# Gated cross-attention block with a two-of-eight expert layer on one core: the order of work on four engines, the pieces of GpSimd's subtractions and the queues of the last stores are changed

## The chip, the cores and the metric

The kernel runs on one core of one Trainium2 chip. The metric is the device time of one launch in microseconds (us). The core's engines run side by side, each in its own program order, and wait for one another through semaphores: TensorE (PE in the rows; PEld is its weight load), VectorE (DVE), ScalarE (ACT), GpSimd (POOL) and SyncE (SP, which here only issues transfers; SPq, ACTq and POOLq are the queues).

## The reference

2048 tokens of width 256 come in 32 sequences of 64. `ctx` has the same shape, no entry is masked, and both gates are scalars.

```python
def xattn(x, ctx):
    q, k_new, v_new = x @ wq.T, x @ wk.T, x @ wv.T
    k, v = concat([ctx, k_new]), concat([ctx, v_new])      # per sequence: 64 old and 64 new keys
    return softmax(q @ k.T / 16) @ v @ wo.T

def ffn(x):                                                # 8 experts, the 2 best of a softmax router
    combine = top_2(softmax(x @ gate_w.T))
    y = sum_e combine[:, e] * ((silu(x @ fc1[e].T) * (x @ fc2[e].T)) @ proj[e].T)      # width 176
    shared = (silu(x @ s_fc1.T) * (x @ s_fc2.T)) @ s_proj.T                            # width 704
    return y + sigmoid(x @ s_gate.T) * shared

x = x + tanh(g_xattn) * xattn(layernorm(x), ctx)
x = x + tanh(g_ffn) * ffn(layernorm(x))
```

## The kernel before

**Arithmetic.** Every float32 operand of a product is held as two parts, hi and lo. ScalarE writes hi (a copy to the fp32r type, functions whose names end in `_hi`, line 751), and VectorE (functions in `_lo`, line 978) or GpSimd writes lo = value - hi. A product is then three matmuls (hi·hi, hi·lo, lo·hi; `chain`, line 408, and `pj`, line 647). So a result in a PSUM bank goes TensorE, ScalarE, VectorE, TensorE before the next product can use it, and the order of the `_hi` and `_lo` calls in each engine's program says which product gets its operands first. All orders are written out by hand; no scheduler moves anything.

**Attention** (to about 116 us) runs over four chunks c of 512 tokens, each of four tiles j of 128. TensorE's loop interleaves, for chunk c, the scores, the values (`values`: x and ctx times the folded weights), the transposes of the probabilities (`probs_t`), the product of probabilities and values (`attend`), with the projections of chunk c+1 (`project(c+1, i)`, all through bank 3, so that one waits until the `project_lo` before it has emptied the bank), and with the second norm, the router and the routing of chunks c-1 and c-2. `attend(c, j)` needs, in this order, ACT's `probs_hi`, DVE's `v_lo` and DVE's `probs_lo` of tile j. ScalarE's loop also holds what is not needed at once: `first_apply(c+2)` (four scalings of x by the first norm, line 783), `second_apply(c, p)` (two scalings by the second norm, line 788) and `shared_hi(c)` (hi of a piece of the shared weights). VectorE's holds `two_best(c)` (the two best experts of each token, and in its last lines the counts per expert, ending in `v_oh`) and `slots(c)` (slot numbers). GpSimd writes lo of the cached keys (`cached_lo`, line 1434) and of the shared weights (line 1467), computes the norms' factors, and scatters tokens to their experts' slots in DRAM (line 1447).

**Shared layer, first part** (115 to 196 us). PRE = 3 of the four chunks s, six blocks j each: `fc(s, j)` (12 matmuls of 512 columns; 6 for j = 5), `s_silu` (ACT, line 912), `s_mult` (DVE, line 1301), `s_hi` (ACT), `s_lo` (DVE), `pj(s, j)` (12 matmuls of 256 columns; 8 for j = 5). TensorE runs `pj` two blocks behind `fc`. `s_sums(s)` (DVE, line 1323) scales the four sums of chunk s out of the banks that `pj(s+1, 0)` overwrites. Between the blocks, at the places of `PIECE_AT`, ten pieces of expert weights are loaded, split by ACT and DVE (`expert_weights`, two buffers, so SP loads piece n when piece n-2 is done). `slots(LAST)` stands at block (0, 5) and is followed by the three parts of `tile_table` (which expert owns which tile of 128 slots), at the places of `TABLE_AT`; its end, `v_eid`, lets SP write padding rows and TensorE read an expert's number.

**Experts** (196 to 278 us): 39 tiles of 128 slots in a software pipeline, `e_step(s)`: TensorE does the up product of tile s (6 matmuls), a transpose for tile s-1 (line 727), the input transposes `xx` of tile s+2 (line 692), the down product of tile s-2; GpSimd adds the result rows to `y2_d` in DRAM.

**End** (278 to 306 us): the last chunk's shared blocks; eight loads of the summed rows; `combine(n)` (DVE, line 1288, adds the two halves for two tiles, in the chunk order 3, 0, 1, 2); `s_sums(3)` (line 1326); stores of three chunks (SP, line 393) and four single tiles (SP, line 396), each after its part is written.

## Time and profile before

| | |
|---|---|
| median of 3 runs | 308.07 us (307.22 to 308.78) |
| the profiled execution | 307.5 us, of which the span of its instructions is 305.7 us |
| granted TensorE clock | 0.998 of full (2.4 GHz) |
| busy: PE / DVE / ACT / POOL | 90% / 71% / 56% / 42% of the span |
| DMA | 40.18 MB, mean 131 GB/s |

How to read it: all times in the rows are us from the span's start. A row of the timeline is start, duration, engine, line, operation, output and inputs by the program's names with their shapes, and, where the engine stood idle first, in brackets how long and what released it. Matmuls overlap in a row's durations: one of 512 columns is followed by the next after 0.23 us, one of 256 after 0.12 us. The names of tiles are those of the storage: `work` is a scratch tile with many views, and a view of `ew_hi` in attention is an operand, not an expert's weight.

### The profile page before, as it was taken

What the parts mean: (1) busy time and instruction counts of PE and PEld (TensorE: products, weight loads), DVE (VectorE), ACT (ScalarE), POOL (GpSimd) and SP (SyncE); (2) the same over time, 40 slices, a digit from 0 to 9 for tenths busy, and PEclk for the clock granted to TensorE, in tenths of its full rate; (3) what the DMA queues carried; (4) which work ended last, traced back from release to release, by engine and by line L of the source; (5) the groups of instructions that cost most, each with busy time, mean ns of one, the idle gap of its engine ahead of it and who ended that gap; (6) DMA issues with size and microseconds to landing.
All of it is one profiled execution on the core that took longest, in us unless ns stands there. A gap on an engine that the chain in (4) does not pass through costs nothing.

```text
span 305.7 us, 5847 instructions
## 1 busy us (share of the span) xinstructions
PE 276.5 (90%) x1785; PEld 247.2 (81%) x1785; DVE 216.7 (71%) x698; ACT 170.2 (56%) x399; POOL 129.0 (42%) x146
## 2 busy tenths in 40 slices
PE   3987989989988889799899999799999999999991
PEld 3876778778877767599788888699999999998871
DVE  3866866869968957666866776877777777764384
ACT  1776577768565455555225456366666666654230
POOL 3412431431684245732432000038777877775000
PEclk9999999999999999999999999999999999999999
DMA  7470226112036021524234575158888888755896
GB/s 205 162 244 2 71 87 191 69 51 71 28 94 235 20 89 70 183 86 119 95 125 135 184 250 164 34 143 142 138 141 139 131 138 137 121 69 69 272 343 210
DMA packets 30494, 40.18 MB, mean 131 GB/s; under 512 B 2944, under 2 KB 26624, under 8 KB 30464
## 3 DMA queue, kind: packets, MB, share of 16 engines
q1 hardware_dynamic: 22880, 30.05, 31.3%
q0 software_dynamic: 7152, 9.57, 18.6%
q8 instruction: 15, 0.25, 0.3%
q10 hardware_dynamic: 432, 0.18, 0.3%
q14 instruction: 15, 0.12, 0.1%
HBM read 22.68 MB, written 17.11 MB: 130 GB/s over the span
## 4 chain that ended last, share of the span: by engine, by line
PE 42%; DVE 23%; issue 12%; ACT 10%; DMA 7%; POOL 4%; SPq 1%; DVEq 0%; POOLq 0%; ACTq 0%
PE bank L408 32%; PE bank L647 4%; DVE ew_lo L978 4%; ACT ew_hi L751 3%; DMA ew_hi<-y_d 3%; PE bank L727 2%; PE bank L692 2%; DVE xt_lo L978 2%; DVE work L1301 2%; DVE neg_max L1022 2%; POOL y_d L1484 2%; ACT work L783 1%; DMA xn_all<-x_dram 1%; ACT sh_hi L751 1%; DMA y_d<-work,dest_of_slot 1%
## 5 line engine op out<-in xcount | busy, mean ns | idle before, releaser
L1484 POOL DMA_INDIRECT y_d<-work,dest_of_slot x39 | 60.6, 1553 | 56.4 <-DVE dest_of_slot L1374 54.1
L408 PE MATMUL bank<-ew_hi,xt_hi 128*128 (+2 forms) x172 | 53.8, 322 | 0.5 <-issue 0.5
L408 PE MATMUL bank<-ew_lo,xt_hi 128*128 (+2 forms) x172 | 51.8, 301 | 0.0
L408 PE MATMUL bank<-ew_hi,xt_lo 128*128 (+1 forms) x133 | 40.5, 305 | 0.0
L978 DVE TENSOR_TENSOR xt_lo<-bank,xt_hi 128x256 fp32r<-128x256 f32 (+2 forms) x90 | 35.7, 398 | 2.9 <-ACT xt_hi L751 1.5
L1447 POOL DMA_INDIRECT xs_d<-xn_all,slot_of_pair x32 | 32.2, 1007 | 10.1 <-issue 7.0
L408 PE MATMUL bank<-ew_hi 128*128 128x256 f32 (+1 forms) x100 | 30.9, 316 | 4.4 <-ACT ew_hi L751 2.8
L408 PE MATMUL bank<-xt_hi,sw_hi 128*128 128x512 f32 x88 | 34.6, 393 | 0.0
L408 PE MATMUL bank<-xt_lo,sw_hi 128*128 128x512 f32 x88 | 34.5, 392 | 0.0
L751 ACT ACTIVATE xt_hi<-bank 128x256 fp32r<-128x256 f32 (+1 forms) x90 | 32.7, 409 | 3.1 <-PE bank L416 1.6
L408 PE MATMUL bank<-xt_hi,sw_lo 128*128 128x512 f32 x88 | 34.3, 390 | 0.0
L978 DVE TENSOR_TENSOR ew_lo<-bank,ew_hi 128x512 fp32r<-128x512 f32 (+1 forms) x41 | 22.6, 581 | 16.4 <-ACT ew_hi L751 12.2
L408 PEld LDWEIGHTS bank<-ew_hi,xt_hi 128*128 128x128 f32 (+1 forms) x172 | 32.4, 188 | 0.9 <-issue 0.7
L408 PEld LDWEIGHTS bank<-ew_lo,xt_hi 128*128 128x128 f32 (+1 forms) x172 | 32.7, 190 | 0.1
L408 PE MATMUL bank<-ew_lo,ew_hi 128*128 128x256 f32 (+1 forms) x100 | 30.2, 309 | 2.5 <-DVE ew_lo L978 2.3
L408 PE MATMUL bank<-ew_hi,ew_lo 128*128 128x256 f32 (+1 forms) x100 | 30.3, 310 | 1.2 <-DVE ew_lo L978 1.2
L647 PE MATMUL bank<-sw_hi,sh_hi 128*128 128x256 f32 x96 | 27.0, 286 | 3.2 <-DVE sh_hi L978 2.2
L751 ACT ACTIVATE sh_hi<-work 128x512 fp32r<-128x512 f32 (+1 forms) x24 | 15.2, 632 | 25.7 <-DVE work L1301 20.4
L912 ACT ACTIVATE work<-bank 128x512 f32<-128x512 f32 (+1 forms) x24 | 14.3, 595 | 22.8 <-PE bank L408 21.6
L647 PE MATMUL bank<-sw_lo,sh_hi 128*128 128x256 f32 x96 | 26.6, 282 | 0.0
L408 PEld LDWEIGHTS bank<-ew_hi 128*128 128x128 f32 x100 | 18.7, 188 | 7.9 <-ACT ew_hi L751 5.2
L751 ACT ACTIVATE ew_hi<-bank 128x512 fp32r<-128x512 f32 (+1 forms) x45 | 21.6, 516 | 6.2 <-PE bank L416 2.1
(159 smaller groups left out, 685.2 us busy)
## 6 DMA issues: line engine op xcount, KB each, us to landing
work<-xs_d SPq DMA_DIRECT2D x39, 136.0 KB
weight_stage<-ew_dram SPq DMA_DIRECT2D x10, 486.5 KB, 4.1
ew_hi<-y_d SPq DMA_DIRECT2D x8, 512.0 KB, 7.9
y_d<-work SPq DMA_DIRECT2D x6, 512.0 KB, 4.4
work<-ctx_t_dram SPq DMA_DIRECT2D x4, 512.0 KB, 3.5
xn_all<-x_dram SPq DMA_DIRECT2D x3, 512.0 KB, 5.1
out_dram<-xn_all SPq DMA_DIRECT2D x3, 512.0 KB, 3.4
xs_d<-pad_row SPq DMA_DIRECT2D x9, 136.0 KB, 1.8
```

The source lines that it names most:

```text
L408: last = nc.tensor.matmul(dst, a, b, start=(n == 0), stop=(n == len(pairs) - 1))
L647: last = nc.tensor.matmul(B[4 + t][:, 0:D], h[:, t * P:(t + 1) * P], w, start=(j == 0 and n == 0), stop=(j == S_FULL and n == len(parts) - 1))
L692: last = nc.tensor.transpose(B[w % 2][:, k * P:(k + 1) * P], EX[:, w, k * P:(k + 1) * P], ident)
L727: last = nc.tensor.transpose(B[4 + v][:, i * P:(i + 1) * P], EH[:, v, i * P:(i + 1) * P], ident)
L751: return nc.scalar.activation(dst, src, ACT.Copy, scale=scale)
L783: nc.scalar.activation(XA[:, j, :], XNR[:, c * TPC + j, :], ACT.Identity, bias=nb1[:, j:j + 1], scale=rs1[:, j:j + 1]).then_inc(a_xn, 1)
L912: nc.scalar.activation(STH[0:rows, j % 2, :], B[pair(s, j)][0:rows, :], ACT.Silu).then_inc(a_th, 1)
L978: return nc.vector.tensor_tensor(dst, src, hi.bitcast(F32), ALU.subtract)
L1022: last = nc.vector.tensor_reduce(nmx[r, j % 2:j % 2 + 1], own_keys(B[4 + j % 2], b), mybir.AxisListType.XY, ALU.max, negate=True)
L1301: nc.vector.tensor_tensor(SHF[0:rows, j % 2, :], STH[0:rows, j % 2, :], h2, ALU.mult).then_inc(v_h, 1)
L1447: nc.gpsimd.indirect_dma_start(out=xs_d, out_offset=bass.IndirectOffsetOnAxis(ap=POS[:, i, n:n + 1], axis=0), in_=XN[:, n, :], in_offset=N ...
L1484: nc.gpsimd.indirect_dma_start(out=y2_d, out_offset=bass.IndirectOffsetOnAxis(ap=IX[:, n:n + 1], axis=0), in_=EY[:, n % 4, :], in_offset=None,
```

## The change

1. ScalarE, attention: `shared_hi(c)` moves from before the conversions of tile 2 to behind them; `second_apply(c, 0)` from before the conversions of tile 3 to the chunk's end.
2. VectorE, attention: the last four operations of `two_best` become `counts(c)`, which runs behind `probs_lo(c, 0)`; TensorE's `route(c-2)` moves behind `values(c, 1)`.
3. GpSimd: each subtraction of 512 columns of the cached keys is cut into two, each of 768 columns of weights into four.
4. VectorE, shared layer: the head of the tile table moves from block (0, 5) to (1, 0), and every part of the table stands behind `s_sums`.
5. Start of the experts: the first two input transposes stand before `pj(2, 4)`, in banks 2 and 3 (before: behind `pj(2, 4)`, in banks 0 and 1), the up product of tile 0 stands between `pj(2, 4)` and `pj(2, 5)`, their conversions (`e_step(-2)`) before `s_hi(2, 5)` and `s_lo(2, 5)`, and VectorE's clearing of `EH` behind `s_lo(2, 0)`.
6. End: `combine(4)` behind `s_lo(3, 4)`; the store of chunk 2 in two halves; stores alternate between SP's and ACT's queue.

```diff
-TABLE_AT = ((0, 5), (1, 1), (1, 2))
+TABLE_AT = ((1, 0), (1, 1), (1, 2))
...
+            sp.wait_ge(v_c2, 2 * N_CH - 1)
+            at = (LAST - 1) * TPC
+            sp.dma_start(out_c[LAST - 1][:, 0:2, :], XNR[:, at:at + 2, :]).then_inc(d_out, 16)
+            for t in range(LAST * TPC + 1, N_T, 2):
                 sp.wait_ge(v_z, t + 1)
                 sp.dma_start(out_t[t], XNR[:, t, :]).then_inc(d_out, 16)
...
                 attend(c, 0)
+                values(c, 1)
                 if c > 1:
                     route(c - 2)
-                values(c, 1)
...
                 for n in range(ahead, len(order) + 2):
-                    if n == len(order) + 1 and s1 == PRE:
-                        pe.wait_ge(v_h, 6 * PRE)
+                    if n == len(order) and s1 == PRE:
+                        pe.wait_ge(v_h, 6 * PRE - 1)
                         xx(0, 0, 16)
                         xx(1, 1, 16)
+                    if n == len(order) + 1 and s1 == PRE:
+                        pe.wait_ge(ew_lo, E_PIECES)
+                        pe.wait_ge(v_eid, 1)
+                        up(0, 0)
                     if n >= 2:
                         pj(*order[n - 2])
...
                 exps(c, 3)
-                if c < LAST:
-                    shared_hi(c)
                 if c > 0:
                     logits(c - 1)
                 v_hi(c, 2)
                 probs_hi(c, 2)
+                if c < LAST:
+                    shared_hi(c)
...
                 if c + 2 < N_CH:
                     first_apply(c + 2)
-                second_apply(c, 0)
                 v_hi(c, 3)
                 probs_hi(c, 3)
                 if c < LAST:
                     project_hi(c + 1, 3)
+                second_apply(c, 0)
...
+            at = (LAST - 1) * TPC + 2
+            act.wait_ge(v_c2, 2 * N_CH)
+            act.dma_start(out_c[LAST - 1][:, 2:4, :], XNR[:, at:at + 2, :]).then_inc(d_out, 16)
+            for t in range(LAST * TPC, N_T, 2):
+                act.wait_ge(v_z, t + 1)
+                act.dma_start(out_t[t], XNR[:, t, :]).then_inc(d_out, 16)
...
                 probs_lo(c, 0)
+                if c > 1:
+                    counts(c - 2)
...
+                    if (s, j) == (PRE - 1, S_FULL):
+                        e_step(-2, 2, -1)
+                    s_lo(s, j)
+                    if (s, j) == (PRE - 1, 0):
+                        nc.vector.memset(EH, 0.0)
...
                     if s > 0 and j == 0:
                         s_sums(s - 1)
+                    if (s, j) in TABLE_AT:
+                        tile_table(TABLE_AT.index((s, j)))
...
                 s_mult(LAST, j)
-                if j == 4:
-                    combine(4)
                 s_lo(LAST, j)
                 if j == 4:
+                    combine(4)
                     combine(5)
...
                 for k in range(KD):
-                    last = nc.gpsimd.tensor_tensor(keys[1][:, k, :, OLD, :], CR[:, k, :].rearrange("p (j n) -> p j n", j=TPC),
-                                                   keys[0][:, k, :, OLD, :].bitcast(F32), ALU.subtract)
+                    for j in (0, 2):
+                        last = nc.gpsimd.tensor_tensor(keys[1][:, k, j:j + 2, OLD, :],
+                                                       CR[:, k, j * P:(j + 2) * P].rearrange("p (j n) -> p j n", j=2),
+                                                       keys[0][:, k, j:j + 2, OLD, :].bitcast(F32), ALU.subtract)
...
+                    for q in range(4):
+                        at = slice(q * SW_PIECE // 4, (q + 1) * SW_PIECE // 4)
+                        to = slice(c * SW_PIECE + at.start, c * SW_PIECE + at.stop)
+                        last = nc.gpsimd.tensor_tensor(SW[1][:, to], STF[:, at], SW[0][:, to].bitcast(F32), ALU.subtract)
```

ScalarE's program at the end of chunk 1, before: the rows are `project_hi(2, 2)`, `first_apply(3)`, `second_apply(1, 0)`, `v_hi`, `probs_hi` of tile 3, `project_hi(2, 3)`, and the conversions of the next chunk.

```order
L751 ACTIVATE ew_hi<-bank 128x4x128
L783 ACTIVATE work<-xn_all,ln_bias,ln_rstd 128x256 x4
L788 ACTIVATE xn_all<-work,ln_bias,ln_rstd 128x256 x2
L751 ACTIVATE ew_hi<-bank 128x512
L751 ACTIVATE ew_hi<-bank 128x256
L751 ACTIVATE ew_hi<-bank 128x4x128
L751 ACTIVATE xt_hi<-bank 128x2x256 x2
```

The same place in the changed kernel:

```order
L769 ACTIVATE ew_hi<-bank 128x4x128
L801 ACTIVATE work<-xn_all,ln_bias,ln_rstd 128x256 x4
L769 ACTIVATE ew_hi<-bank 128x512
L769 ACTIVATE ew_hi<-bank 128x256
L769 ACTIVATE ew_hi<-bank 128x4x128
L806 ACTIVATE xn_all<-work,ln_bias,ln_rstd 128x256 x2
L769 ACTIVATE xt_hi<-bank 128x2x256 x2
```

The two scalings of line 788 (806 in the changed kernel) went from before three conversions to behind them.

VectorE's program from the end of `slots(3)` at block (0, 5) on, before: seven small operations are the head of the table, then come `s_mult(1, 0)`, `s_lo(1, 0)`, `s_sums(0)` and `s_mult(1, 1)`.

```order
L1137 COPY work<-work 128x8
L1152 TENSOR_TENSOR work<-work 1x8
L1153 CAST end_of_expert<-work 1x8
L1155 TENSOR_TENSOR work<-work 1x128
L1157 TENSOR_REDUCE work<-work 1x8
L1158 SCALAR_TENSOR_TENSOR work<-work 1x8
L1160 TENSOR_SCALAR work<-work 1x8
L1161 MEMSET work 1x1
L1301 TENSOR_TENSOR work<-work,bank 128x512
L978 TENSOR_TENSOR sh_lo<-work,sh_hi 128x512
L1323 TENSOR_SCALAR work<-bank,shared_gate 128x256 x4
L1301 TENSOR_TENSOR work<-work,bank 128x512
```

The same place in the changed kernel:

```order
L1165 COPY work<-work 128x8
L1332 TENSOR_TENSOR work<-work,bank 128x512
L1002 TENSOR_TENSOR sh_lo<-work,sh_hi 128x512
L1354 TENSOR_SCALAR work<-bank,shared_gate 128x256 x4
L1180 TENSOR_TENSOR work<-work 1x8
L1181 CAST end_of_expert<-work 1x8
L1183 TENSOR_TENSOR work<-work 1x128
L1185 TENSOR_REDUCE work<-work 1x8
L1186 SCALAR_TENSOR_TENSOR work<-work 1x8
L1188 TENSOR_SCALAR work<-work 1x8
L1189 MEMSET work 1x1
L1332 TENSOR_TENSOR work<-work,bank 128x512
```

The head went behind `s_sums(0)`, so `s_mult(1, 0)` follows `slots(3)` at once.

TensorE's program in the changed kernel from the last matmul of `fc(2, 5)` to the second half of the first up product (three rows of `pj(2, 4)` stand for its twelve):

```order
L415 MATMUL bank<-xt_hi,sw_lo 128x512
L703 MATMUL bank<-consts_sb,work 128x128 x4
L654 MATMUL bank<-sw_hi,sh_hi 128x256
L654 MATMUL bank<-sw_lo,sh_hi 128x256
L654 MATMUL bank<-sw_hi,sh_lo 128x256
...
L708 TENSOR_LOAD expert_of_tile
L709 ISA
L712 ISA
L415 MATMUL bank<-ew_hi,xt_hi 128x352
...
L654 MATMUL bank<-sw_hi,sh_hi 128x256
L654 MATMUL bank<-sw_lo,sh_hi 128x256
```

Before, the four transposes (line 692 there) stood between the two projections, and the up product with its register load behind the second.

## Rows read from the trace of the kernel before

**Rows 1.** Busy time in four stretches (PE, PEld, DVE, ACT, POOL, clock, DMA share, GB/s)

```profile
69.70:84.20 14.50, 13.56 (x94) 11.95 (x94) 13.63 (x53) 10.08 (x29) 6.66 (x10) 1.00 0.15 54
94.90:105.90 11.00, 9.21 (x69) 8.19 (x68) 10.14 (x45) 6.54 (x20) 2.59 (x7) 1.00 0.17 61
...
200.00:278.00 78.00, 78.00 (x577) 76.58 (x576) 57.40 (x258) 50.81 (x150) 58.69 (x38) 1.00 0.78 125
303.00:304.00 1.00, 0.00 (x0) 0.00 (x0) 0.00 (x0) 0.00 (x0) 0.00 (x0) 1.00 1.05 351
```

**Rows 2.** Timeline at the end of chunk 0

```profile
40.18 1.08 ACT L788 ACTIVATE xn_all<-work,ln_bias,ln_rstd 128x256 f32<-128x256 f32 x2
...
42.06 0.38 PE L408 MATMUL bank<-ew_hi 128*128 128x256 f32 x1 [0.98 <-ACT ew_hi L751]
```

**Rows 3.** Timeline at the end of chunk 1

```profile
65.05 1.08 ACT L788 ACTIVATE xn_all<-work,ln_bias,ln_rstd 128x256 f32<-128x256 f32 x2
...
66.92 0.38 PE L408 MATMUL bank<-ew_hi 128*128 128x256 f32 x1 [0.85 <-ACT ew_hi L751]
```

**Rows 4.** Timeline: VectorE's line 1094 in chunk 1, and in chunk 2

```profile
62.24 0.19 DVE L1094 TENSOR_TENSOR work<-logits,work 128x32 f32<-128x32 f32 x1
...
87.33 1.86 POOL L1467 TENSOR_TENSOR sw_lo<-weight_stage,sw_hi 128x768 fp32r<-128x768 f32 x1
...
87.48 1.75 DVE L1094 TENSOR_TENSOR work<-logits,work 128x32 f32<-128x32 f32 x1
...
90.75 0.51 PE L408 MATMUL bank<-xt_hi,ew_hi 128*128 128x512 f32 x1 [0.83 <-DVE sw_lo L978]
```

**Rows 5.** Groups of GpSimd's instructions, shapes apart

```profile
L1467 POOL TENSOR_TENSOR sw_lo<-weight_stage,sw_hi 128x768 fp32r<-128x768 f32 x3 | 5.6, 1851 | 0.0
L1434 POOL TENSOR_TENSOR ew_lo<-work,ew_hi 128x512 fp32r<-128x512 f32 x4 | 5.1, 1295 | 10.8 <-ACT ew_hi L751 10.8
```

**Rows 6.** Timeline of TensorE in chunk 3: `attend(3, 0)` and `attend(3, 1)`

```profile
99.86 0.39 PE L408 MATMUL bank<-ew_lo,ew_hi 128*128 128x256 f32 x1 [1.15 <-DVE ew_lo L978]
...
105.47 0.39 PE L408 MATMUL bank<-ew_hi,ew_lo 128*128 128x256 f32 x1 [0.55 <-DVE ew_lo L978]
```

**Rows 7.** Timeline: head of the table, first matmul of `pj(1, 0)`

```profile
147.73 0.15 DVE L1152 TENSOR_TENSOR work<-work 1x8 f32<-1x8 f32 x1
...
152.10 0.36 PE L647 MATMUL bank<-sw_hi,sh_hi 128*128 128x256 f32 x1 [1.01 <-DVE work L1323]
```

**Rows 8.** Timeline of VectorE: `s_sums(1)`

```profile
174.58 1.66 DVE L1323 TENSOR_SCALAR work<-bank,shared_gate 128x256 f32<-128x256 f32 x4
```

**Rows 9.** The chain that ended last, 172 to 200 us

```profile
176.29 0.70 DVE work L1301
...
179.83 3.62 DMA weight_stage<-ew_dram
...
194.73 0.48 DVE work L1376
```

**Rows 10.** Timeline at the start of the experts

```profile
194.71 0.36 PE L647 MATMUL bank<-sw_hi,sh_hi 128*128 128x256 f32 x1 [0.82 <-DVE sh_hi L978]
...
196.26 1.65 DVE L1323 TENSOR_SCALAR work<-bank,shared_gate 128x256 f32<-128x256 f32 x4
...
198.42 0.30 PE L727 MATMUL bank<-consts_sb,work 128*128 128x128 f32 x1 [0.28 <-DVE work L1361]
```

**Rows 11.** Timeline of the end: `combine(4)`, `pj(3, 4)`, `pj(3, 5)`

```profile
295.59 0.69 DVE L1288 TENSOR_TENSOR xn_all<-ew_hi 128x512 f32<-128x512 f32 x1 [0.99 <-DMA ew_hi<-y_d]
...
296.94 0.39 PE L647 MATMUL bank<-sw_hi,sh_lo 128*128 128x256 f32 x1 [0.64 <-DVE sh_lo L978]
...
299.74 0.35 PE L647 MATMUL bank<-sw_hi,sh_hi 128*128 128x256 f32 x1 [1.34 <-DVE sh_hi L978]
```

**Rows 12.** The stores of line 396: durations of an issue (ns), first and last start

```profile
L396 SPq DMA_DIRECT2D out_dram<-xn_all x4: 404/450/878, 301.5 to 303.3; - x4
```

**Rows 13.** Timeline of VectorE: the last four sums

```profile
300.95 1.66 DVE L1326 SCALAR_TENSOR_TENSOR xn_all<-bank,shared_gate,xn_all 128x256 f32<-128x256 f32 x4
```

More of the change, by code:

```diff
@@ L702, in e_step @@
                     fc(PRE, 0, (1,))
[L703 to L708 removed]
+                if live(s, 0) and s > 0:
+                    fcs = upper(s, u)
                 if live(s, 2):
@@ L714, in e_step @@
                 if fcs:
-                    last = chain(B[2 + u % 2][:, 0:2 * F_E],
-                                 [(EXT[a][:, u % 2, k, :], fcs[k][b]) for k in range(KD) for a, b in THREE],
-                                 [(0, e_xl, s + 1)])
-                    last.then_inc(e_fc, 1)
+                    up(s, u, fcs)
                 if s == 1:
@@ L1275, in _ @@
             two_best(LAST - 1)
+            counts(LAST - 1)
             def shared_tail_lo(i):
```

129 lines of the change are left out of this document (66 added, 63 removed).

## The prediction

> **What bounds the kernel now.** I read the page first: TensorE is busy for 90% of the span at a granted clock of 0.998, so the time is its matmuls plus the stretches in which it waits, some 30 us in all. The waits were then read from the timeline, one by one, and the chain that ended last showed which of them carry the end. In the expert stage there is none: TensorE is busy for 78.00 of 78 us [rows 1], so nothing that starts the stage differently makes it shorter. The waits lie in attention, at the start of chunk 1 of the shared layer, at the start of the experts and at the end. Each edit aims at one of them, so I take them in the order of the program and ask at each what becomes the last condition once the present one is gone.
>
> **Term 1, second norm behind the conversions (ScalarE).** At the end of chunk 0 `attend(0, 3)` starts at 42.06 after a wait for ScalarE [rows 2]. ScalarE did two scalings from 40.18 on, 1.08 us, and only then `v_hi` and `probs_hi`. Their inputs were ready (the transposes had ended at 39.7). With the scalings behind, both conversions start 0.98 us earlier (the second scaling overlaps by 0.1), VectorE's `v_lo` and `probs_lo` with them, since VectorE was idle there, and the wait of 0.98 shrinks to next to nothing. The two scalings now fall into ScalarE's own idle time before the next chunk's conversions (1.58 us before, 1.08 needed), and their reader, the transposes of the second norm, comes more than 5 us later. Gain 0.97. At the end of chunk 1 the same stands at 65.05 and 66.92 [rows 3]: a wait of 0.85 plus 0.13 of staggered starts, gain 0.95. In chunks 2 and 3 VectorE or TensorE itself is last there and nothing is gained. Bounds: 0 and 1.08 each. `shared_hi` (0.85 us) behind the conversions of tile 2 gains nothing: in chunk 0 VectorE's `v_lo` is the last condition, later on TensorE's own `values`; and it costs nothing, because ScalarE then waits over 1.3 us for VectorE anyway.
>
> **Term 2, GpSimd's pieces.** In chunk 1 VectorE's operation of line 1094 takes 0.19 us; in chunk 2 it took 1.75 and ended with GpSimd's subtraction of 768 columns (87.33, 1.86 us), inside which it had started [rows 4]. Behind it stand ScalarE's `route_exp` and `project_hi(3, 2)`, VectorE's `project_lo(3, 2)` and TensorE's `project(3, 3)`, which needs bank 3 and waited until 90.75. Cut into four, a piece takes about 1.86 / 4 = 0.47 us; if VectorE gets in at the end of a piece, line 1094 ends at about 88.0 in place of 89.23, and TensorE's whole gap there goes: 0.83 us of idle time and 0.25 of pipeline start. Gain 1.08; the next condition, `project_lo(3, 2)` at about 89.4, comes before the transposes are out. Bounds: 0, if the pieces follow each other without letting VectorE in, and 1.56, the whole stretch. The Trainium skill (SBUF — State Buffer, Who interferes with whom) says that a VectorE instruction with two SBUF inputs contends with a GpSimd one that reads SBUF, and that the first to issue holds the shared pair for its whole instruction. The trace agrees with 1.75 against 0.19; by that rule the wait is one piece, 0.47 us, and it does not say who is served next between two pieces.
>
> The pieces also cost. From the two sizes, 1.851 for 768 and 1.295 for 512 columns [rows 5], 256 columns are worth 0.556, so an instruction has a fixed part of about 0.18, of which some 0.15 shows between neighbours. Two more of them stand in `cached_lo(0)` at 12 to 15 us, before the norm factors for which ScalarE, then the folded weights and TensorE's gap at 19.3 wait: loss 0.2 (bounds 0 and 0.4). The other groups are hidden: GpSimd is idle for 5 us and more before them.
>
> **Term 3, counts behind `probs_lo` (VectorE).** `attend(3, 0)` waits 1.15 us for `v_lo(3, 0)` [rows 6], which stood behind the 0.95 us of counts. It will start that much earlier. But VectorE does the same work in the same stretch and has no idle mark from 94.9 to 105.9 (busy 10.14 of 11.0, the rest is the start of small dependent operations) nor from 69.7 to 84.2 (13.63 of 14.5) [rows 1]; `attend(3, 1)` then waits for its `probs_lo` at 105.47 [rows 6] and will wait 0.95 longer. The gain is given back 6 us later, in chunk 2 and in chunk 3. Value taken: 0; bounds 0 and 0.95 each.
>
> **Term 4, head of the table.** At 152.10 `pj(1, 0)` starts, 1.01 us idle and 1.16 late by TensorE's pace, because `s_sums(0)` was late; before it stood the head, from 147.73 to 149.45 [rows 7]. Without it `s_mult(1, 0)` starts at 148.05 (end of its `s_silu`), the hi and lo conversions follow, `s_sums(0)` begins at 150.05 and its first bank is free at 150.5, before TensorE has finished `fc(1, 1)` at 150.94. Gain 1.16. The head (1.72 us) then delays `s_mult(1, 1)` to 153.35 and `s_lo(1, 1)` to 155.4; `pj(1, 1)`, now at 155.25, needs lo with its third matmul at 155.5. That is just in time, and by block (1, 4) VectorE has caught up. If it isn't, some 0.3 of the gain goes. Bounds 0.8 and 1.16. SP has the table's end at 161 and doesn't need it before 165.
>
> **Term 5, start of the experts.** TensorE idles 0.82 us before `pj(2, 5)` [rows 10], and the up product (1.05 us) now fills this gap. What follows is not TensorE's: the first transposes of line 727 at 198.42 wait for VectorE, which does `s_sums(2)` from 196.26 to 197.85 and then the first gated product [rows 10]. `s_sums(2)` needs the end of `pj(2, 5)`, and that now stands behind the up product: lo of block (2, 5) at 194.57, up product until then or later, projection 0.95, so `s_sums(2)` starts at 195.85 at best, 0.4 earlier. Against this stands VectorE's clearing of `EH`, 0.48 us, which moves from 194.73 [rows 9] to just before `s_sums(1)` at 174.58 [rows 8]. That place is on the chain too: `s_mult(2, 1)` at 176.29 follows `s_sums(1)` at once, and from it the chain runs through the load of a weight piece (179.83) and every block to 194.73 [rows 9]. So 0.4 of the 0.48 is paid at the other end. The sum is 0; bounds a gain of 0.8 and a loss of 0.6 (the clearing, and 0.2 if a tile for the first transposes lands late: these now run at 190.8, and the transfers were under way until 191.2).
>
> **Term 6, the end.** `combine(4)` waited for its loads until 295.59 and stood before `s_lo(3, 4)`; `pj(3, 4)` waited 0.64 for that and `pj(3, 5)` 1.34 [rows 11]. With `s_lo` first (at 295.3), the next operations are bound by the loads and by VectorE: two sums to 297.25, `s_mult(3, 5)` there in place of 297.52. So only 0.27 of the two waits is gained. The last sum ends at 302.61 [rows 13], but SP issues its last store at 303.3, since the four issues take 0.40 to 0.88 each [rows 12]. With two queues the last store is issued at 302.4 (0.27 earlier than 302.61, plus a start of 0.05). Gain at the end 0.95 in all; bounds 0.27 and 1.0. The Trainium skill (DMA: Bandwidth & Descriptors, Issuing engines are not separate DMA queues) speaks against it: transfers of all queues share the 16 DMA engines, and a second queue saves only the issue time. By rows the last megabyte moves at 351 GB/s with the engines full [rows 1], 3.0 us; it begins an issue earlier too, since half of chunk 2 goes at 300.0 in place of 300.9.
>
> **Sum.** 0.97 + 0.95 + 1.08 - 0.2 + 0 + 1.16 + 0 + 0.95 = 4.9. The profiled execution took 307.5, which gives 302.6. It lay 0.57 below the median of the three runs, 308.07, so against that the forecast is **303.1 us**.
>
> **Rivals.**
> - *The pieces don't let VectorE in.* For it: one such meeting is all that the trace has. Against: nothing says that GpSimd keeps the ports between instructions. Then term 2 is -0.2 alone: 304.2.
> - *Saturated VectorE takes term 1 too.* In chunks 1 and 2 VectorE is busy for 94% of 69.7 to 84.2 [rows 1]. If that stretch is pinned by something else than its own start, the 1.9 us of term 1 is swallowed, as term 3 is. Against: its start follows `v_lo` of the chunk before without slack. 305.0; together with the first 306.0.
> - *More is gained.* Terms 3 and 5 at their upper bounds, where VectorE's small operations overlap better than I think: 1.2 more, 301.9.
> - *Slower: the expert loop falls into another phase.* The first up product is done before the last projection, and the banks of the first inputs are others, so the loop starts with other distances between its four engines. At present each of its 39 steps takes 2.00 us, GpSimd is busy for 58.69 of 78 us, in steps of 1.86. Should the loop settle at 2.2 us a step, that is 39 x 0.2 = 7.8 us: 310.9. It decides from 0.13 us a step on. Against: TensorE has no gap in it at all [rows 1], so it sets the pace whatever the start.
>
> **How the numbers follow.** Forecast as summed, with small errors (302.2 to 303.9): 0.58. Pieces without effect (304.2): 0.12. Term 1 swallowed or most of several terms (305 to 306.3): 0.14. More (301.3 to 302.1): 0.10. A loss that eats all (306.5 and more, from the experts' start, weight pieces that land late, or the phase): 0.06. The range from 301.7 to 305.6 leaves out the last two parts in most of their width, 0.2 in all. Half a per cent of 308.07 is 1.5 us, about what a measurement of this kernel can tell from no change; faster by more than that means below 306.5: 0.90; the same 0.07; slower 0.03.
>
> **What would show it.** Right: no wait above 0.3 us for ScalarE before the last `attend` of chunks 0 and 1; line 1094 (1118 in the changed kernel) under 0.7 us in chunk 2 and no wait for VectorE in front of `project(3, 3)`; a longer wait in `attend(3, 1)`, about 1.5 us; no gap before `pj(1, 0)`; the distance from `pj(2, 0)` to the experts' first transposes of line 747 unchanged within 0.5; 2.00 us a step; the last store's issue 0.1 us behind the last sum. Wrong: a new wait right behind a removed one, above all for VectorE in blocks (1, 1) and (2, 0), or for a tile's transfer at the first transposes.

## The result and the profile after

The changed kernel took 304.15 us in the median of 4 runs (303.13 to 305.98), the kernel before 308.42 in the same comparison: a ratio of 0.988, 95% interval 0.985 to 0.991. By the ratio that is 3.7 us faster (the two medians lie 4.3 apart), where 5.0 were forecast; the time lies inside the forecast range. A second comparison (the first experiment below) gave 0.994 (0.993 to 0.996), 1.7 us by the ratio. So what the change gives is smaller than forecast on both, and the two intervals do not meet.

The profiled execution took 305.98 us with a span of 304.2, so only 1.5 us less than the profiled one of before (span 305.7). To see where, I compare starts that both traces have. "exps c" is ScalarE's first exponential of chunk c, "silu s, j" the start of `s_silu(s, j)`, all read from the timeline. The last two columns are kernels of the experiments.

| start, us | before | changed | whole keys | all favoured |
|---|---|---|---|---|
| `project(0, 0)` | 10.78 | 12.63 | 11.08 | 10.25 |
| exps 0 | 20.97 | 23.55 | 21.28 | 19.90 |
| exps 0, tile 2 | 28.99 | 32.68 | 29.27 | 27.89 |
| exps 1 | 46.89 | 49.58 | 46.17 | 44.79 |
| exps 1, tile 2 | 53.38 | 56.07 | 52.67 | 51.28 |
| exps 2 | 70.82 | 72.58 | 69.17 | 67.73 |
| exps 2, tile 2 | 77.69 | 79.31 | 75.89 | 74.60 |
| exps 3 | 95.49 | 96.06 | 92.58 | 91.30 |
| silu 0, 0 | 119.56 | 119.97 | 118.02 | 115.81 |
| silu 1, 1 | 151.13 | 151.52 | 149.57 | 147.34 |
| silu 1, 3 | 160.77 | 160.39 | 158.43 | 155.70 |
| silu 3, 0 | 277.94 | 277.30 | 275.43 | 272.69 |
| last four sums | 300.95 | 300.03 | 298.16 | 294.91 |
| end of the span | 305.7 | 304.2 | 302.3 | 299.1 |

From line to line of the table, before against changed: 1.85 lost ahead of the first projection (the first loads landed later: in the twelve profiles of the experiments this start lies anywhere from 10.2 to 11.7, so I take it for chance), 0.73 and 1.11 lost in the first two stretches of chunk 0 (the second one is the clock's: e2_weights_whole, with the same pieces of the keys and no fall of the clock there, takes 8.03 us for it, 8.02 before, 9.13 here), then 1.00, 0.93, 1.05 + 0.14 and 0.16 gained in attention, 0.77 at the start of chunk 1, 0.26 up to the last chunk, 0.28 and 0.6 at the end. The gains make 5.2 us, where 5.1 were forecast (4.9, and the 0.2 of loss that was set against them); what was not forecast is the start.

The start of the changed kernel, from the timeline (start, duration, engine, line, operation):

```profile
14.12 3.28 POOL L1468 TENSOR_TENSOR ew_lo<-work,ew_hi 128x256 fp32r<-128x256 f32 x4 [4.48 <-ACT ew_hi L769]
...
19.56 1.09 ACT L801 ACTIVATE work<-xn_all,ln_bias,ln_rstd 128x256 f32<-128x256 f32 x2 [1.85 <-POOL ln_bias L1443]
20.56 1.06 ACT L769 ACTIVATE ew_hi<-bank 128x512 fp32r<-128x512 f32 x2
...
21.91 0.38 PE L415 MATMUL bank<-ew_hi 128*128 128x256 f32 x1 [2.04 <-DVE ew_lo L1002]
```

GpSimd's `cached_lo(0)` takes 3.28 us (two instructions of 1.29 before). Behind it come the norm's factors, for them ScalarE's scalings wait (line 801), behind the scalings stands `project_hi(0, 3)`, and TensorE's first scores wait for its lo until 21.91. They are now 9.28 us behind `project(0, 0)`, where it was 8.55. And TensorE's clock then fell: busy time by engine (PE, PEld, DVE, ACT, POOL), the granted clock, DMA share and GB/s of that stretch and of the expert stage:

```profile
22.84:26.21 3.37, 3.37 (x18) 3.37 (x17) 1.15 (x4) 1.81 (x8) 0.00 (x0) 0.51 0.44 155
200.00:278.00 78.00, 78.00 (x576) 76.52 (x575) 57.06 (x257) 51.46 (x150) 58.99 (x38) 1.00 0.79 123
```

The clock of the first row is the lower level of 1.2 GHz; before, it had been 2.4 there throughout. TensorE had stood idle for 2.04 us by its mark, and had worked for about 1 us again when the clock fell. Matmuls of 256 columns follow one another every 0.21 us in place of 0.12 in this stretch. The expert stage is what it was [rows 1].

The places of the other terms in the changed kernel, VectorE's line 1118 (the line 1094 of before: durations min/median/max) and TensorE's waits:

```profile
L1118 DVE TENSOR_TENSOR work<-logits,work x4: 193/212/478, 64.9 to 130.6; 128x32 f32<-128x32 f32 x4
```

```profile
44.75 0.38 PE L415 MATMUL bank<-ew_hi 128*128 128x256 f32 x1
...
68.67 0.38 PE L415 MATMUL bank<-ew_hi 128*128 128x256 f32 x1
...
99.47 0.39 PE L415 MATMUL bank<-ew_lo,ew_hi 128*128 128x256 f32 x1 [0.21 <-DVE ew_lo L1002]
...
104.46 0.35 PE L415 MATMUL bank<-ew_hi 128*128 128x256 f32 x1 [0.73 <-DVE work L1165]
...
105.89 0.39 PE L415 MATMUL bank<-ew_hi,ew_lo 128*128 128x256 f32 x1 [0.55 <-DVE ew_lo L1002]
...
156.15 0.39 PE L654 MATMUL bank<-sw_hi,sh_lo 128*128 128x256 f32 x1 [0.22 <-DVE sh_lo L1002]
...
197.92 0.30 PE L747 MATMUL bank<-consts_sb,work 128*128 128x128 f32 x1 [1.02 <-DVE work L1365]
...
298.82 0.36 PE L654 MATMUL bank<-sw_hi,sh_hi 128*128 128x256 f32 x1 [1.94 <-DVE sh_hi L1002]
```

The waits of [rows 2] and [rows 3] are gone (44.75 and 68.67, no mark of idle time). Line 1118 takes at most 0.48 us. In chunk 3 the wait of 1.15 [rows 6] has become 0.21, and 0.73 stands in front of `attend(3, 1)` in its place. At 156.15 a small wait is new: `pj(1, 1)`. At 298.82 `pj(3, 5)` waits 1.94 (1.34 before), while the 0.64 of `pj(3, 4)` is gone [rows 11].

### The profile page after: what moved, and what is told of

Read it like the earlier page. It is cut to its first block, busy times and chain, and to the rows that moved or that the text cites. A ratio compares the mean times of both kernels' runs of the same rounds, so it can differ in the third digit from the quotient of the medians.

```text
span 304.2 us, 5865 instructions
## 1 busy us (share of the span) xinstructions
PE 276.9 (91%) x1785; PEld 249.0 (82%) x1785; DVE 215.7 (71%) x698; ACT 170.6 (56%) x399; POOL 131.1 (43%) x163
## 4 chain that ended last, share of the span: by engine, by line
PE 55%; DVE 23%; ACT 8%; issue 6%; POOL 3%; DMA 3%; DVEq 0%; ACTq 0%; SPq 0%; POOLq 0%
PE bank L415 43%; PE bank L654 6%; DVE ew_lo L1002 4%; ACT ew_hi L769 3%; PE bank L747 3%; DVE work L1332 3%; PE bank L703 3%; DVE xt_lo L1002 2%; ACT sh_hi L769 2%; DMA consts_sb<-consts_dram 2%; DVE work L1354 2%; DVE neg_max L1046 2%; ACT work L801 1%; DVE sh_lo L1002 1%; DMA weight_stage<-ew_dram 1%
## 5 line engine op out<-in xcount | busy, mean ns | idle before, releaser
L415 PE MATMUL bank<-ew_hi,ew_lo 128*128 128x256 f32 (+1 forms) x100 | 31.1, 318 | 1.5 <-DVE ew_lo L1002 1.5
L415 PEld LDWEIGHTS bank<-ew_hi 128*128 128x128 f32 x100 | 19.5, 196 | 7.0 <-ACT ew_hi L769 3.7
```

The lines of the kernel that those rows point to most:

```text
L415: last = nc.tensor.matmul(dst, a, b, start=(n == 0), stop=(n == len(pairs) - 1))
```

## The experiments

All but the first and the last take one step from the changed kernel or from the kernel with whole keys; the last, e10_best, takes six. Each was timed beside the kernel before. By the table's differences a local effect is read to 0.05 us, while the executions of one kernel lie 1.4 to 3.8 us apart. Much of that goes with TensorE's clock: in every one of these kernels the executions with a lower granted clock tended to be the slower ones (in e2_weights_whole 304.5 and 305.0 at 0.993, 307 at 0.981). So the verdicts on local effects rest on the traces, and the medians are given for what they can carry.

**e0_same: the changed kernel again.** No edit.

> The changed kernel once more, unaltered, to see which part of the 3.7 us that it had lost by 29 us is chance. Theory A: the first loads landed 1.85 us later by chance, GpSimd's longer cached_lo(0) cost 0.73 us, and TensorE's clock fell to half behind the idle time of 2.2 us that this left, which cost 1.1 us. Then cached_lo(0) again takes 3.28 us against 2.55 in the kernel before, and the clock falls again between 22 and 27 us; the ratio to the kernel before is 0.985 to 0.991. Rival: the fall of the clock was chance too. Then the granted clock stays at 1.00 there, and the ratio is 0.983 to 0.987.

305.61 us (304.58 to 306.35) against 307.43, ratio 0.994 (0.993 to 0.996). `cached_lo(0)` took 3.29 us, TensorE again waited 2.04 us for the first scores, until 20.85, and the clock fell again (0.80 in 20 to 22 us, 0.50 in 22 to 24). Theory A by the trace, though the ratio lies above its range of 0.985 to 0.991, interval and all. The six executions had a granted clock of 0.981 to 0.991, 0.985 in the mean, the four of the first comparison 0.986 to 0.996, 0.990 in the mean: the clock fell more often here.

**e1_keys_whole: the cached keys in 512 columns again.**

```diff
-                    for j in (0, 2):
-                        last = nc.gpsimd.tensor_tensor(keys[1][:, k, j:j + 2, OLD, :], ...
+                    last = nc.gpsimd.tensor_tensor(keys[1][:, k, :, OLD, :], CR[:, k, :].rearrange("p (j n) -> p j n", j=TPC),
+                                                   keys[0][:, k, :, OLD, :].bitcast(F32), ALU.subtract)
```

> Only the cached keys are subtracted in 512 columns again (two instructions in place of four a chunk); the weights stay in pieces. Theory A: cached_lo(0) is back at 2.55 us, the norm's factors come 0.73 us earlier, TensorE's idle time before the second projection of chunk 0 falls from 2.2 to about 1.4 us, and its clock stays at 1.00 from 22 to 27 us. So 0.7 to 1.8 us faster than the changed kernel, a ratio of 0.982 to 0.986 to the kernel before. Rival: the late first loads alone made the start slow; then the time is that of the changed kernel within 0.3 us. The gain at project(3, 3) in chunk 2 stays in either case if the pieces of the weights made it.

303.87 us (302.31 to 304.78), ratio 0.988 (0.986 to 0.990): 1.7 us faster than the changed kernel beside it, with intervals that do not meet. That is theory A's gain, at a ratio above the 0.982 to 0.986 that it gave, as the changed kernel's beside it was above its own. The timeline at the same places:

```profile
12.57 2.56 POOL L1467 TENSOR_TENSOR ew_lo<-work,ew_hi 128x512 fp32r<-128x512 f32 x2 [4.47 <-ACT ew_hi L769]
...
19.63 0.39 PE L415 MATMUL bank<-ew_hi 128*128 128x256 f32 x1 [1.07 <-DVE ew_lo L1002]
```

The scores stand 8.55 us behind the first projection, as before, and the clock is 1.00 there. So the pieces of the keys cost 0.73 us by themselves in the two traces of the changed kernel, and the kernel as a whole lost more with them than that. But the clock fell in another place, which was not expected (same columns as above):

```profile
102.00:103.00 1.00, 0.59 (x5) 0.59 (x6) 0.84 (x4) 0.11 (x1) 0.70 (x2) 1.00 0.00 0
103.00:104.00 1.00, 1.00 (x6) 0.64 (x5) 0.78 (x2) 0.80 (x4) 0.71 (x1) 0.78 0.37 139
104.00:105.00 1.00, 1.00 (x3) 0.58 (x3) 0.39 (x3) 0.00 (x0) 0.96 (x1) 0.50 0.74 242
...
107.00:108.00 1.00, 1.00 (x10) 0.80 (x9) 0.00 (x0) 0.47 (x1) 0.60 (x2) 1.00 0.16 61
```

It fell behind the two waits that end at 101.0 and 102.4 (0.73 and 0.54 us by their marks; 0.88 and 0.81 when each is counted as the distance between two matmuls less the usual 0.12), for some 3.4 us. From exps 3, tile 2 to silu 0, 0 this trace takes 19.80 us, the changed kernel's 18.28: such a fall costs 1.5 us. Without it this execution's span would have been 300.8.

**e4_norm_between: the norm's factors behind the first half of `cached_lo(0)`.** The keys are in pieces here.

```diff
                 for k in range(KD):
+                    if (c, k) == (0, 1):
+                        rstd1(1)
...
             cached_lo(0)
-            rstd1(1)
```

> Pieces as in the changed kernel, but the norm's factors of chunk 1 stand between the two halves of cached_lo(0), behind its first two pieces. The statistics were ready at 15.63 us and the factors began at 17.37. Theory A: factors 1.6 us earlier, and TensorE's idle time before the second projection of chunk 0 shrinks from 2.2 us to under 1.0, without a fall of the clock: 1.2 to 2.5 us faster than the changed kernel, ratio 0.979 to 0.985. Rival: another condition is right behind (the conversions of the first projection, or the scores that now wait for the second half of cached_lo(0)), so that less than 0.7 us is gained.

303.81 us (302.32 to 305.36), ratio 0.990 (0.987 to 0.992), 1.8 less than the changed kernel beside it, with intervals that just do not meet (0.9924 and 0.9926). GpSimd in this trace:

```profile
12.69 1.45 POOL L1470 TENSOR_TENSOR ew_lo<-work,ew_hi 128x256 fp32r<-128x256 f32 x2 [4.33 <-ACT ew_hi L769]
14.66 1.06 POOL L1438 TENSOR_TENSOR ln_bias<-ln_mean_var,consts_sb 128x4 f32<-128x4 f32 x1 [0.53 <-DVE ln_mean_var L1017]
```

The next condition was right behind, as the rival says: GpSimd waits 0.53 us for VectorE's statistics, TensorE's wait is 1.09, and the start is that of whole keys (exps 0 at 21.25). It gives back what the pieces cost and no more: the 1.8 us of the medians are in theory A's range, but the trace shows 0.86 from the first projection to exps 0, and the rest can be the clock's, which did not fall at the start here. The first operation of the factors takes 1.06 us where it takes 0.19 in the changed kernel: it started just behind the start of VectorE's clearing (14.63) and ended with VectorE's subtraction (15.03, 0.63 us).

**e2_weights_whole: the weights in 768 columns again**, one instruction in place of the loop over q.

> Only the weights are subtracted in 768 columns again (one instruction in place of four a chunk); the cached keys stay in pieces. Theory A: the pieces of the weights made the gain of 1.1 us before project(3, 3). VectorE's line 1118 takes over 1 us in chunk 2 again, TensorE waits about 0.8 us for VectorE before project(3, 3) at some 91 us, and the kernel is about 1.1 us slower than the changed one, ratio 0.989 to 0.994. Rival: the earlier work of VectorE (counts behind probs_lo) moved line 1118 out of the meeting anyway. Then line 1118 stays under 0.3 us and the time is that of the changed kernel within 0.3 us.

306.70 us (304.49 to 307.23), ratio 0.996 (0.994 to 0.998), 1.1 slower than the changed kernel beside it. VectorE's line 1118, and TensorE at `project(3, 3)`:

```profile
L1118 DVE TENSOR_TENSOR work<-logits,work x4: 192/192/1741, 62.7 to 129.4; 128x32 f32<-128x32 f32 x4
```

```profile
90.10 0.51 PE L415 MATMUL bank<-xt_hi,ew_hi 128*128 128x512 f32 x1 [0.84 <-DVE sw_lo L1002]
```

Theory A by the trace: one operation of 1.74 us, and from exps 2, tile 2 to exps 3 it takes 17.83 us against 16.73 in e0_same. The ratio is above the expected 0.989 to 0.994, again as e0_same's was.

In this run `cached_lo(0)` took 3.69 us. The lines of GpSimd on the keys (durations in ns, min/median/max) of the changed kernel and of this one show why the cost is not a fixed one:

```profile
L1468 POOL TENSOR_TENSOR ew_lo<-work,ew_hi x8: 725/740/1192, 14.1 to 57.8; 128x256 fp32r<-128x256 f32 x8
```

```profile
L1468 POOL TENSOR_TENSOR ew_lo<-work,ew_hi x8: 732/736/1589, 12.5 to 55.6; 128x256 fp32r<-128x256 f32 x8
```

The long one is the fourth piece in both (16.21 and 14.61). In the changed kernel it started just behind VectorE's subtraction of two SBUF inputs (16.09, 0.72 us) and took 1.19 in place of 0.74; in this run VectorE's clearing and the subtraction stood there:

```profile
14.58 0.48 DVE L1233 MEMSET work<- 128x512 f32 x1
14.98 0.63 DVE L1002 TENSOR_TENSOR ew_lo<-weight_stage,ew_hi 128x512 fp32r<-128x512 f32 x1
...
14.61 1.59 POOL L1468 TENSOR_TENSOR ew_lo<-work,ew_hi 128x256 fp32r<-128x256 f32 x1
```

In both the piece ended 0.6 us behind the end of the subtraction. But in this run it had started 0.37 us before the subtraction did, while the clearing ran; whether the clearing held it up until then is not shown. The scores stand 10.12 us behind the first projection here; e7_one_queue, with whole keys and a start 0.37 earlier, has 9.10, so the pieces cost 1.0 us in this run.

**e9_counts_back: `counts` back in `two_best`,** with whole keys; `route` stays behind `values(c, 1)`.

> The kernel with whole keys (the run before), and in it counts(c) back in two_best, ahead of v_lo(c, 0). In the run with whole keys two waits of TensorE, 0.88 and 0.81 us, stand 1.4 us apart in chunk 3 at 101 to 102.5 us, and behind them its clock fell to half from 103.2 to 107 us, which cost 1.5 us; five of its six runs had a granted clock of 0.986 or 0.987, one 0.997, and that one was 1.5 us faster. Theory A: with counts in its old place the waits lie 5 us apart again (near 98.5 and 104), the clock falls there in fewer runs, and against the kernel with whole keys 0 to 1.2 us is gained, although 0.15 us of waits comes back; ratio to the kernel before 0.984 to 0.988. Rival: the fall there is chance. Then the clock of the runs is spread as with whole keys, and the time is 0.1 to 0.3 us longer.

304.73 us (303.04 to 305.45), ratio 0.987 (0.984 to 0.990). TensorE in chunk 3:

```profile
99.20 0.38 PE L415 MATMUL bank<-ew_lo,ew_hi 128*128 128x256 f32 x1 [1.16 <-DVE ew_lo L1002]
...
103.83 0.36 PE L415 MATMUL bank<-ew_hi 128*128 128x256 f32 x1 [0.36 <-DVE work L1165]
...
105.26 0.39 PE L415 MATMUL bank<-ew_hi,ew_lo 128*128 128x256 f32 x1 [0.54 <-DVE ew_lo L1002]
```

The trace had no fall in chunk 3, but one at 27.5 us, and the granted clock of the five executions was 0.988 to 0.994, 0.990 in the mean, against 0.989 with whole keys: that the clock falls less often this way is not shown. And the waits add up to more than in either kernel: from exps 3 to silu 0, 0 it takes 24.51 us, 24.07 before and 23.91 in the changed kernel. `route` behind `values(3, 1)` makes the slot numbers late, and `attend(3, 1)` waits for them (line 1165); with `counts` in its new place the shorter wait at `attend(3, 0)` pays for that, here nothing does. The trace agrees with the theory in one thing, the fall in chunk 3 was absent, at a price of 0.6 in place of 0.15; the ratio, 0.987 against 0.988 with whole keys, decides nothing.

**e5_clear_early: the clearing of `EH` behind `s_lo(1, 4)`,** with whole keys.

```diff
-                    if (s, j) == (PRE - 1, 0):
+                    if (s, j) == (1, 4):
                         nc.vector.memset(EH, 0.0)
```

> The kernel with whole keys, and in it the clearing of EH behind s_lo(1, 4) in place of behind s_lo(2, 0). Theory A: in the changed kernel the clearing delayed s_sums(1) and cost 0.28 us at pj(2, 0) and pj(2, 1); in block (1, 4) VectorE has free time, so the distance from pj(1, 5) to the first product of the experts shrinks by 0.28 us. Rival: the weight pieces set the pace of blocks (2, 1) to (2, 4), and the distance stays the same within 0.1.

303.88 us (303.61 to 305.28), ratio 0.987 (0.984 to 0.990). From silu (2, 1) to silu (2, 2) the trace takes 4.22 us against 4.47 with whole keys: 0.25 gained. To the experts' first transposes and to silu (3, 0) 0.15 of it is left, between the 0.28 of theory A and the 0.1 of its rival. So the clearing did cost there, and the experts' start gives a part back.

**e6_table_later: the table's parts one block later,** with whole keys: `TABLE_AT = ((1, 1), (1, 2), (1, 3))`.

> The kernel with whole keys, and in it the three parts of the tile table one block later each, at (1, 1), (1, 2) and (1, 3). Theory A: the head between s_sums(0) and s_mult(1, 1) made pj(1, 1) late by 0.38 to 0.5 us; behind s_lo(1, 1) it costs nothing, so the distance from pj(1, 0) to fc(1, 3) shrinks by 0.4 to 0.5 us. Rival: the delay comes from s_sums(0) itself, or the table's end, then near 165 us, holds back SP's padding rows and with them a piece of expert weights, and what is gained at pj(1, 1) is lost before the experts start.

304.45 us (302.44 to 305.37), ratio 0.986 (0.983 to 0.990). From silu (1, 1) to (1, 3) it takes 8.36 us against 8.86: the 0.5 of theory A. But from there to (1, 5) it takes 7.44 against 7.00, and TensorE has the same small wait two blocks on:

```profile
165.72 0.39 PE L654 MATMUL bank<-sw_hi,sh_lo 128*128 128x256 f32 x1 [0.20 <-DVE sh_lo L1002]
```

Part three, from 161.00 to 162.60, now met the first weight piece of chunk 1 on VectorE (162.53, 1.15 us). Neither theory had this one: the loss was moved, not removed.

**e8_combine_late: `combine(5)` behind `s_mult(3, 5)`,** with whole keys.

```diff
+                if j == 5:
+                    combine(5)
                 s_lo(LAST, j)
...
                     combine(4)
-                    combine(5)
```

> The kernel with whole keys, and in it combine(5) behind s_mult(3, 5) in place of behind combine(4). Theory A: VectorE's order is all that holds pj(3, 5); s_mult(3, 5) starts 0.5 us earlier, combine(5) hides in the time in which ScalarE writes hi, TensorE's wait before pj(3, 5) shrinks from 2.1 to 1.6 us and the last sum ends 0.5 us earlier, the span with it. Rival: the last transfers are bound by the DMA engines, which move 340 to 370 GB/s from the first store of the last part on; then the last sum is 0.5 us earlier and the distance from it to the end grows by as much.

303.39 us (301.78 to 305.46), ratio 0.985 (0.981 to 0.988). VectorE at the end:

```profile
293.03 0.69 DVE L1332 TENSOR_TENSOR work<-work,bank 64x512 f32<-64x512 f32 x1
293.64 0.68 DVE L1319 TENSOR_TENSOR xn_all<-ew_hi 128x512 f32<-128x512 f32 x1
294.41 0.69 DVE L1002 TENSOR_TENSOR sh_hi<-work,sh_hi 64x512 fp32r<-64x512 f32 x1
295.13 1.30 DVE L1319 TENSOR_TENSOR xn_all<-ew_hi 128x512 f32<-128x512 f32 x2
296.46 1.66 DVE L1357 SCALAR_TENSOR_TENSOR xn_all<-bank,shared_gate,xn_all 128x256 f32<-128x256 f32 x4
```

`pj(3, 5)` waits 1.44 in place of 1.94, the last sums start 4.06 us behind silu (3, 5) in place of 4.56, and the distance from them to the end stays 4.14. Theory A: 0.5 us.

**e3_seconds_back: `second_apply(c, 0)` back before `v_hi(c, 3)`,** with whole keys.

> The kernel with whole keys, and in it second_apply(c, 0) back before v_hi(c, 3). Theory A (term 1 as forecast): TensorE waits about 0.9 us for ScalarE before attend(0, 3) and attend(1, 3) again, and from the first scores of chunk 2 on everything is 1.9 us later by the trace, nothing of it given back; in time 1.9 us slower than with whole keys. Rival: the stretch of saturated VectorE that follows swallows a part of it, so the shift at the first scores of chunk 3 is under 1.2 us.

304.61 us (304.21 to 305.62), ratio 0.991 (0.987 to 0.994).

```profile
42.28 0.39 PE L415 MATMUL bank<-ew_hi 128*128 128x256 f32 x1 [0.96 <-ACT ew_hi L769]
...
67.14 0.38 PE L415 MATMUL bank<-ew_hi 128*128 128x256 f32 x1 [0.83 <-ACT ew_hi L769]
```

Both waits are back, exps 2 is 1.96 us later against its first projection than with whole keys, exps 3 1.95: nothing is swallowed. Theory A, within 0.1 by the trace. The ratios differ by 0.7 us only, with intervals that meet; the clock of these executions was higher (0.992 in the mean, 0.989 with whole keys).

**e7_one_queue: all stores on SP's queue, chunk 2 still in halves,** with whole keys.

```diff
+            for h in range(2):
+                sp.wait_ge(v_c2, 2 * N_CH - 1 + h)
+                sp.dma_start(out_c[LAST - 1][:, 2 * h:2 * h + 2, :], ...
-            for t in range(LAST * TPC + 1, N_T, 2):
+            for t in range(LAST * TPC, N_T):
```

> The kernel with whole keys, and in it all stores on SP's queue, those of chunk 2 in halves as now. Theory A: an issue takes 0.37 to 0.6 us on a queue, so with six on one queue the last one is issued 0.6 to 0.8 us later, and the distance from the start of the last four sums to the end of the span grows from 4.1 us to about 4.7. Rival (one queue more saves nothing, the transfers share the DMA engines): that distance stays within 0.2 us.

303.46 us (301.71 to 305.52), ratio 0.986 (0.981 to 0.990). Its issues, and VectorE's last sums:

```profile
298.94 0.98 SPq L401 DMA_DIRECT2D out_dram<-xn_all x2
300.06 1.89 SPq L404 DMA_DIRECT2D out_dram<-xn_all x4
```

```profile
299.55 1.66 DVE L1352 SCALAR_TENSOR_TENSOR xn_all<-bank,shared_gate,xn_all 128x256 f32<-128x256 f32 x4
```

From the last sums to the end of the span (303.7) it is 4.15 us, with two queues 4.14. The rival is right: the second queue gives nothing.

**e11_project_first: ScalarE's `project_hi(0, 3)` before `first_apply(1, (0, 1))`,** with whole keys.

> The kernel with whole keys, and in it ScalarE's project_hi(0, 3) before first_apply(1, (0, 1)). With whole keys TensorE waits 1.23 us before the first scores, because project_hi(0, 3) stands behind two scalings that wait for GpSimd's factors. Theory A: that wait goes, the scalings start 0.35 us later, the first exponentials 0.9 us earlier, and 0.9 us is kept to the end. Rival: the next wait, 2.38 us for the conversions of the next chunk's input, hangs on the scalings and not on the scores; then it grows by what was won and less than 0.3 us is left.

302.78 us (302.32 to 304.72), ratio 0.986 (0.981 to 0.990). TensorE at the first scores and at the next wait:

```profile
18.26 0.39 PE L415 MATMUL bank<-ew_hi 128*128 128x256 f32 x1 [0.25 <-DVE ew_lo L1002]
...
24.10 0.30 PE L498 MATMUL bank<-consts_sb,work 128*128 128x128 f32 x1 [1.87 <-DVE xt_lo L1002]
```

The wait before the scores is 0.25 in place of 1.07, and the next one stays (1.87, 1.85 with whole keys). The run beside it whose first projection starts at the same time is e7_one_queue (10.22, here 10.18): its exps 0 is at 20.96, here at 19.90, so 1.0 us is won, and from exps 0 to exps 1 it takes 24.92 us, 24.89 with whole keys: nothing is given back. Against e1_keys_whole, whose first projection starts 0.9 later, the distance from projection to exps 0 is 0.48 shorter (9.72 against 10.20), so between 0.5 and 1.0 is won, by when the first loads land. Theory A. This trace had the fall in chunk 3 again (0.77 in 100 to 102 us, 0.50 in 102 to 104).

**e10_best: what was favoured, together.** Whole keys, `project_hi(0, 3)` first, `counts` back, the clearing at (1, 4), the table at (1, 1), (1, 2), (1, 2), `combine(5)` late.

> What the runs so far favour, together: whole keys, project_hi(0, 3) first, counts back in two_best, the clearing of EH behind s_lo(1, 4), the table's parts at (1, 1), (1, 2), (1, 2), combine(5) behind s_mult(3, 5). Against the kernel with whole keys: 0.9 at the start, -0.3 for the counts, 0.15 for the clearing, 0.5 for the table (in block (1, 2) no weight piece stands beside it), 0.5 at the end, and fewer falls of the clock in chunk 3, up to 1 us: 1.7 to 2.7 us faster, ratio to the kernel before 0.976 to 0.983. Rival: the table's two parts in one block make block (1, 3) late by 0.5 us, and the clock falls as often; then 1.2 us.

301.38 us (300.65 to 303.74), ratio 0.981 (0.976 to 0.985). The last column of the table is this kernel. It gains 0.5 at the table and gives 0.2 back by silu (1, 5), 0.5 at the end, and had no fall in chunk 3; `pj(3, 5)` waits 1.45. It is the fastest here by the median; its interval lies below that of e0_same and of e1_keys_whole, and ends where the first comparison's begins, at 0.985. Against whole keys the ratios give 2.3 us, inside the expected 1.7 to 2.7.

## Why the prediction was right, and where it was not

**The result lay in the range, but the gain was smaller than the forecast 5.0:** 3.7 us in the first comparison, 1.7 in the second. By the traces that comes from the start, not from the terms that gain. There is luck in it too: in the second comparison the same kernel took 305.61 us, at the very edge of the range (305.6), and gained less than the 2.5 us that this edge stands for.

**Term 1: right.** Forecast 0.97 + 0.95; the table has 1.00 + 0.93, and e3_seconds_back takes both away again. The rival "saturated VectorE takes term 1 too" is refuted by the same run.

**Term 2, the weights: right.** Forecast 1.08, measured 1.05 in the changed kernel and 1.10 by e2_weights_whole. VectorE does get in between the pieces, here behind the first:

```profile
88.98 2.28 POOL L1505 TENSOR_TENSOR sw_lo<-weight_stage,sw_hi 128x192 fp32r<-128x192 f32 x4
...
89.15 0.48 DVE L1118 TENSOR_TENSOR work<-logits,work 128x32 f32<-128x32 f32 x1
```

A piece takes 0.61 us, though, not the forecast 1.86 / 4 = 0.47, which left out the fixed part.

**Term 2, the keys: the step that failed.** "From the two sizes ... an instruction has a fixed part of about 0.18 ... loss 0.2 (bounds 0 and 0.4)". Measured: 0.73 by the trace, outside the bounds. The fixed part was about right: a piece takes 0.74 and follows the one before after 0.70, so four make 2.84 in place of 2.55, 0.29; two more pieces at the prediction's own 0.15 would have been 0.3, not 0.2. The missing 0.45 is that the fourth piece met VectorE's subtraction and ended 0.6 us behind it. The meeting itself was not new: before, it fell on the first operation of the norm's factors (0.64 us in place of 0.19), and in the changed kernel the second of them meets VectorE's next such operation for as much (0.64). I had counted on pieces to let VectorE in, and did not count what that means the other way: between two pieces GpSimd can lose its place, and here GpSimd was on the path and VectorE was not. The rule weighed in the prediction (the Trainium skill, SBUF — State Buffer, Who interferes with whom) names both directions; the changed kernel's traces show the second with 1.19 against 0.74. The 1.59 of e2_weights_whole does not follow from it, since there the piece had started ahead of the subtraction.

**What no term had: the clock.** The start's longer wait was followed in both profiles of the changed kernel, though not in that of e2_weights_whole (2.20 us idle, clock 1.00), by a fall to 1.2 GHz, for 1.11 us of loss in the first one. I had read the granted clock of 0.998 as a property of the kernel; it is one of an execution: the kernel before, too, has executions from 0.987 or 0.988 up to 0.998 in each comparison of the experiments. The gain of 1.7 us in e1_keys_whole is the 0.73 and, it seems, fewer such falls: its granted clock was 0.0040 higher in the mean than e0_same's, and in these two kernels' own executions 0.01 of clock goes with 1.2 to 1.7 us, which gives an estimate of 0.5 to 0.7. The rest, 0.3 to 0.5, is inside the scatter.

**Term 3: nearly right.** Forecast 0; 0.14 in chunk 2 and 0.16 in chunk 3. The wait did move to `attend(3, 1)` as forecast, to 0.73 before its first matmul, beside the 0.55 that stood before its third already [rows 6], because `slots` came later and not only `probs_lo`.

**Term 4: mechanism right, size off.** Forecast 1.16 with "if it isn't, some 0.3 of the gain goes"; measured 0.77, just under the lower bound of 0.8. The gap before `pj(1, 0)` is gone (1.28 won from silu 1, 1 to 1, 2), and 0.51 is given back in the next block: the head delays `s_mult(1, 1)` to 154.01 (forecast 153.35, and this trace was 0.39 later at silu 1, 1) and `pj(1, 1)` waits at 156.15. e6_table_later shows the give-back to be the head's place, and that a later place gives it back as well.

**Term 5: right in sum and parts.** Forecast 0; measured 0.26. From silu 2, 1 to 2, 2 the clearing loses 0.28 at its new place, of which e5_clear_early wins 0.25 back, and from there to the experts' first transposes 0.42 is won (0.4 and 0.4 forecast).

**Term 6: right in size, wrong in cause.** Forecast 0.27 + 0.68; measured 0.28 + 0.6. But "With two queues the last store is issued at 302.4" is not what gave the 0.6: e7_one_queue has one queue and the same distance to the end. What is left of the edit is the store of chunk 2 in halves; that is by elimination, no run puts the whole store back. Whole, it was issued at 300.9, with the last sums; as halves, the first goes 0.6 us ahead of the last sums (298.94 against 299.55 in that run), and the transfers of the last megabyte begin that much earlier. The rule that I had set against the term (the Trainium skill, DMA: Bandwidth & Descriptors, Issuing engines are not separate DMA queues) was the right one: with one queue the last store is issued 1.95 us behind the last sums' start, with two 1.69, and the end comes at the same distance.

**The slower rival** did not come: 2.00 us a step, TensorE busy for 78.00 of 78.

## What to carry to other kernels

Cutting an instruction of one engine so that its neighbour gets in has a price that depends on which of the two is on the path there: it paid where VectorE was waited for and cost 0.73 to 1.0 us where GpSimd was. So cut the instruction where the meeting is, not every one of its kind. A second queue at the end is worth only what the issues cost beyond the transfers: when the engines move 350 GB/s to the last byte, an earlier start of the first bytes is the likelier gain. And price the cover of the smallest term with the same care: the one forecast at a loss of 0.2 cost 0.7 us, and 1.8 where the clock fell behind it, of the 5.2 us that the rest brought.

## What the runs showed that was not expected

TensorE's clock falls to 1.2 GHz for 3 to 4 us in some executions of the same kernel and, by the granted clocks, not in others (0.987 in four executions with whole keys, 0.997 in another, which was 1.5 us faster). In the thirteen profiles of changed kernels it fell between 20 and 30 us in five, each time after a wait of 2.04 us, or of 1.1 and 1.9 us (six profiles with these two waits, the one of before among them, and one with 2.20 us have no fall there), and between 100 and 108 us in four, after the two waits in front of and in `attend(3, 1)`; the profile of the kernel before has neither, though its other executions have granted clocks down to 0.987. A fall cost 1.1 to 1.6 us at the first place and 1.5 at the second by the distances. The four were among the eleven with `counts` in its new place, none among the two with it in its old one, but the other seven have the same two waits and no fall, so what decides remains open. In all fourteen it fell at the end too, behind the wait before `pj(3, 5)` or as TensorE ran out of work, and cost nothing that the distances show: from silu (3, 5) to the last sums it is 4.56 us with the fall before them (e7_one_queue, at 299.2) and with the fall behind them (e0_same, at 301.1).
